# The stretch between attention and the expert tiles in another order

## The reference

```
x = x + layernorm(attention(layernorm(x)))
x = x + layernorm(ffn(layernorm(x)))

# ffn: 7 routed experts of width 512, the best 2 of each token, and one shared
logits = x_flat @ router_w.T
top_vals, top_idx = top_k(logits, 2);  top_w = softmax(top_vals)
mixed = sum over the 2 of top_w * swiglu_expert(x_flat)
mixed = mixed + swiglu_shared(x_flat)
```

## Time and profile before

| | us |
|---|---|
| median of 3 runs | 486.38 |
| lowest and highest run | 486.29, 487.9 |
| the profiled execution | 487.31 |
| its span, first to last instruction | 485.5 |

### The profile page before, as it was taken

The page is one execution under the profiler, slowest core; times in us unless marked ns, Lnnn a source line. Parts: engine busy times, 40 slices in busy tenths (PEclk is TensorE's granted clock), DMA queues, the critical chain, the costliest instruction groups (busy, mean ns, idle before and its releaser), DMA issues. The chain is left out here.

```text
span 485.5 us, 10662 instructions
## 1 busy us (share of the span) xinstructions
PE 416.2 (86%) x3980; PEld 255.0 (53%) x3980; DVE 325.7 (67%) x823; ACT 244.5 (50%) x416; POOL 133.8 (28%) x220
## 2 busy tenths in 40 slices
PE   1869899999999999999989878897999999999500
PEld 0533433435243433435244364655699999999500
DVE  5899978797988888797963936499433333333277
ACT  1531167776777677686776707653233233233240
POOL 8200000100111110100110013334667766763332
PEclk9985589999999999999998959999999999999955
DMA  7554750303021020000000017100577687877152
GB/s 218 198 180 142 244 160 20 90 2 88 3 63 28 11 81 2 2 2 4 1 3 3 0 53 208 44 2 0 169 216 248 209 253 247 238 221 239 43 161 86
DMA packets 46694, 50.77 MB, mean 105 GB/s; under 512 B 5363, under 2 KB 34420, under 8 KB 46644
## 3 DMA queue, kind: packets, MB, share of 16 engines
q1 hardware_dynamic: 43632, 44.77, 30.1%
q0 software_dynamic: 2432, 4.99, 3.6%
q10 hardware_dynamic: 580, 0.33, 0.3%
HBM read 36.90 MB, written 12.98 MB: 103 GB/s over the span
## 5 line engine op out<-in xcount | busy, mean ns | idle before, releaser
L640 ACT ACTIVATE probs<-banks 128x1024 f32<-128x1024 f32 (+1 forms) x192 | 145.3, 810 | 59.1 <-PE banks L495 48.0
L786 DVE TENSOR_REDUCE mx_part<-banks 128x1 f32<-128x512 f32 (+2 forms) x224 | 130.2, 646 | 15.9 <-PE banks L476 7.5
L470 PE MATMUL banks<-k_st,q_st 64*128 64x512 bf16 (+3 forms) x384 | 115.7, 354 | 8.0 <-DVE parts L754 4.2
L488 PE MATMUL banks<-q_st,k_st 64*128 64x512 bf16 (+3 forms) x384 | 97.5, 333 | 6.2 <-ACT probs L640 5.9
L507 PE MATMUL banks<-probs,v_pad 128*32 128x512 f32 (+3 forms) x768 | 83.3, 506 | 0.0
L1525 DVE TENSOR_TENSOR hidden<-banks,gate 128x512 f32<-128x512 f32 x38 | 26.3, 692 | 66.2 <-PE banks L1192 66.2
L488 PEld LDWEIGHTS banks<-q_st,k_st 64*128 64x128 bf16 x384 | 31.1, 95 | 60.9 <-ACT probs L640 49.0
L786 DVE TENSOR_REDUCE mx<-banks 128x1 f32<-128x512 f32 (+3 forms) x96 | 51.9, 596 | 16.5 <-PE banks L476 15.2
L470 PEld LDWEIGHTS banks<-k_st,q_st 64*128 64x128 bf16 x384 | 34.4, 95 | 36.3 <-DVE mx_part L786 27.7
L474 PE MATMUL banks<-mask_qk,ident_half 64*128 64x128 bf16 x256 | 52.6, 231 | 0.0
L493 PE MATMUL banks<-mask_kq,ident_half 64*128 64x128 bf16 x256 | 49.3, 221 | 0.0
(11 more groups left out here) (199 smaller groups left out, 572.2 us busy)
## 6 DMA issues: line engine op xcount, KB each, us to landing
w_g<-in_w_gate SPq DMA_DIRECT2D x38, 256.0 KB
w_u<-in_w_up SPq DMA_DIRECT2D x38, 256.0 KB
q_st<-q_rows SPq DMA_DIRECT2D x32, 128.0 KB, 2.9
k_st<-k_rows SPq DMA_DIRECT2D x32, 128.0 KB, 2.9
w_d<-in_w_down SPq DMA_DIRECT2D x8, 256.0 KB, 5.1
back<-results SPq DMA_DIRECT2D x8, 256.0 KB, 4.7
q_rows<-parts SPq DMA_DIRECT2D x4, 384.0 KB, 3.0
k_rows<-parts SPq DMA_DIRECT2D x4, 384.0 KB, 3.5
```

Source lines behind the costliest of these rows:

```text
L470: last = nc.tensor.matmul(dst[:, at:at + width], q_st[r][rows, c, p, (i % CH) * P:(i % CH + 1) * P], k_st[r][rows, kc, p, 0:width], start= ...
L488: last = nc.tensor.matmul(dst[a][:, 0:width], k_st[r][rows, j // CH, p, (j % CH) * P:(j % CH + 1) * P], q_st[r][rows, c, p, first:BANK], s ...
L640: nc.scalar.activation(probs[unit % PROBS][:, 2 * p:2 * p + 2, first:BANK], slot_pair[k % 2].rearrange("p (a t) -> p a t", a=2)[:, :, 0:BA ...
L786: nc.vector.tensor_reduce(dst, taken[:, :, 0:width], AX.X, ALU.max, negate=True).then_inc(max_taken, 1)
```

## The change

- **End of the first block.** The turns and the routing of batch 0 go to the second block (`first_turn_tokens`, `first_route`, their copies and the logits are gone from the first). VectorE inverts the last group's first sums ahead of the second norm and the last ones right behind x2. NEWTON is 3 instead of 4. ScalarE ends its queue with one more square root of a column nobody reads.
- **Second block.** TensorE turns and routes chunks 0 and 1 behind the projection of batch 1 and ahead of any shared unit; ScalarE copies them. Batch 0's logits have a bank of their own. VectorE takes the statistics of batch 1's projection half by half, and the choice is a function of the batch, `choose(b)`, run for 0 and then 1. The shared units stand elsewhere: three of chunk 0 ahead of chunk 2's and 3's turns, the down projection of each chunk later, three of chunk 2 behind the table. ScalarE has one more unread square root ahead of the second root.
- **Last chunk.** `shared_up(3)`, `shared_take(3)`, `shared_last` and `shared_down(3)` stand behind the tiles; ScalarE copies the result between its scaling of chunk 2 and chunk 3, and GpSimd's adds wait for it. `turn(0)` now stands in front of `shared_down(2)`.

```diff
 RSQRT_BITS = float(0x5F3759DF)
-NEWTON = 4
+NEWTON = 3
 E, HID = 7, 512
...
-            def first_turn_tokens():
-                for q in range(2):
-                    pe.wait_ge(x2_ready, q + 1)
-                    for j in range(CH):
-                        last = nc.tensor.transpose(first_x2_bank[q][:, j * P:(j + 1) * P],
-                                                   x2[:, q * CH + j, :], ident[:, :])
-                    last.then_inc(x2_transposed, 1)
-
-            def first_route():
-                pe.wait_ge(x2_t_ready, 2)
-                for t in range(KT):
-                    last = nc.tensor.matmul(first_lg_bank[:, t * 8:t * 8 + E], x2_t[:, t, :], router_sb[:, :],
-                                            start=True, stop=True)
-                last.then_inc(first_logits_done, 1)
-
             pe.wait_ge(parts_ready, 8)
...
             turn_outputs(GROUPS - 1, 1)
-            first_turn_tokens()
-            first_route()
...
             take_outputs(GROUPS - 1, 1)
+            nc.scalar.activation(std[:, KT:KT + 1], ident[:, 0:1], ACT.Sqrt)
...
                                     ).then_inc(vector_steps, step.one())
+            invert_sums(GROUPS - 1, 0)
             dve.wait_ge(vector_steps, step.now())
...
                     last.then_inc(x2_ready, 1)
-            for q in range(2):
-                dve.wait_ge(x2_transposed, q + 1)
-                nc.vector.tensor_copy(x2_t[:, q * CH:(q + 1) * CH, :].rearrange("p t c -> p (t c)"),
-                                      first_x2_bank[q]).then_inc(x2_t_ready, 1)
-            dve.wait_ge(first_logits_done, 1)
-            nc.vector.tensor_copy(logits[:, 0:KT, 0:E],
-                                  first_lg_bank[:, 0:KT * 8].rearrange("p (t e) -> p t e", e=8)[:, :, 0:E]
-                                  ).then_inc(vector_steps, step.one())
-            invert_sums(GROUPS - 1, 0)
             invert_sums(GROUPS - 1, 1)
...
-            lg_bank, t_out = t_bank[:, 0:cut], t_bank[:, 2 * P:2 * P + 3 * TILES]
+            lg_bank, t_out = [d_bank[:, 0:cut], t_bank[:, 0:cut]], t_bank[:, 2 * P:2 * P + 3 * TILES]
             total_bank = t_bank[:, cut:cut + E * NT]
...
                         pool.wait_ge(weighted, n + 1)
+                        pool.wait_ge(s_down_taken, q + 1)
                         nc.gpsimd.tensor_tensor(mixed[:, part, :], mixed[:, part, :], back[i][:, part, :],
...
                     pe.wait_ge(x2_ready, q + 1)
+                    if q >= 2:
+                        pe.wait_ge(x2_t_ready, q - 1)
                     for j in range(CH):
...
                     for t in range(q * CH, (q + 1) * CH):
-                        last = nc.tensor.matmul(lg_bank[:, t * 8:t * 8 + E], x2_t[:, t, :], router_sb[:, :],
+                        last = nc.tensor.matmul(lg_bank[q // QC][:, t * 8:t * 8 + E], x2_t[:, t, :], router_sb[:, :],
                                                 start=True, stop=True)
...
+                turn_tokens(0)
+                turn_tokens(1)
+                route(0)
+                route(1)
                 pe.wait_ge(shared_loaded, 16 * 3)
                 pe.wait_ge(proj_ready, 2)
-                shared_up(0, range(HT))
-                shared_up(1, [0])
-                shared_down(0)
-                shared_up(1, [1])
+                shared_up(0, [0, 1, 2])
                 turn_tokens(2)
...
                 route(3)
-                shared_up(1, [2, 3])
-                shared_up(2, [0])
-
-                pe.wait_ge(picked_ready, 1)
+                shared_up(0, [3])
+                shared_up(1, [0])
+
+                pe.wait_ge(picked_ready, B)
                 pe.wait_ge(route_consts, 8)
...
                 nc.tensor.matmul(total_bank, ones_b[:, :], flat, start=True, stop=True).then_inc(counted, 1)
-                shared_down(1)
-                shared_up(2, [1, 2, 3])
-                shared_up(3, [0])
-                shared_down(2)
+                shared_down(0)
+                shared_up(1, [1, 2, 3])
+                shared_up(2, [0])
                 for k in range(2 * NT):
+                    if k == NT:
+                        shared_down(1)
                     if k % NT == 0:
...
                 last.then_inc(table_done, 1)
-                shared_up(3, [1, 2, 3])
+                shared_up(2, [1, 2, 3])
...
                 turn(0)
-                shared_down(CHUNKS - 1)
+                shared_down(CHUNKS - 2)
                 turn(1)
...
                 up(0)
-                pe.wait_ge(s_down_taken, CHUNKS)
+                pe.wait_ge(s_down_taken, CHUNKS - 1)
                 for k, e in enumerate(digits(pe)):
...
                     project(k, e)
+
+                shared_up(CHUNKS - 1, range(HT))
+                pe.wait_ge(result_ready, TILES)
+                shared_down(CHUNKS - 1)
...
-                shared_take(0, [0])
+                copy_tokens(0)
+                copy_tokens(1)
                 standard_deviations(0, KT, KT)
-                shared_take(0, [1, 2, 3])
+                shared_take(0, [0, 1])
+                nc.scalar.activation(root_table[:, :], ident[:, 0:1], ACT.Sqrt)
                 standard_deviations(1, KT, KT)
+                copy_tokens(2)
+                copy_tokens(3)
+                shared_take(0, [2, 3])
                 shared_take(1, [0])
                 shared_result(0)
-                shared_take(1, [1])
-                copy_tokens(2)
-                copy_tokens(3)
-                shared_take(1, [2, 3])
+                shared_take(1, [1, 2, 3])
+                act.wait_ge(gap_ready, B)
+                nc.scalar.activation(gap_exp[:, :], gap[:, :], ACT.Exp).then_inc(gap_exp_ready, 1)
                 shared_take(2, [0])
                 shared_result(1)
-                act.wait_ge(gap_ready, 1)
-                nc.scalar.activation(gap_exp[:, :], gap[:, :], ACT.Exp).then_inc(gap_exp_ready, 1)
                 shared_take(2, [1, 2, 3])
-                shared_take(3, [0])
-                shared_result(2)
-                shared_take(3, [1, 2, 3])
...
                         gate_rows(k + 1)
+                shared_take(CHUNKS - 1, range(HT))
                 act.wait_ge(weight_ready, 1)
...
                 for q in range(QC, CHUNKS):
+                    if q == CHUNKS - 1:
+                        shared_result(q)
                     act.wait_ge(returned[q], 32)
...
-                def layer_norm(src, at, count, var_sem, std_sem, n):
+                def layer_norm(src, at, count, var_sem, std_sem, n, halves=None):
...
                     for t in range(at, at + count):
+                        if halves is not None and (t - at) % CH == 0:
+                            dve.wait_ge(halves, (t - at) // CH + 1)
                         nc.vector.bn_stats(stats[:, t, :], src(t)).then_inc(steps, step.one())
...
-                dve.wait_ge(proj_ready, 2)
-                layer_norm(lambda t: proj[:, t - KT, :], KT, KT, post_var_ready, post_std_ready, 1)
+                layer_norm(lambda t: proj[:, t - KT, :], KT, KT, post_var_ready, post_std_ready, 1, proj_ready)
                 for t in range(KT, NT):
...
                         last.then_inc(x2_ready, 1)
-                dve.wait_ge(logits_done, QC)
-                nc.vector.tensor_copy(logits[:, KT:, 0:E],
-                                      lg_bank.rearrange("p (t e) -> p t e", e=8)[:, KT:, 0:E]
-                                      ).then_inc(steps, step.one())
-                done()
-                for t in range(NT):
-                    nc.vector.max(top[:, t, :], logits[:, t, :]).then_inc(steps, step.one())
-                done()
-                nc.vector.tensor_tensor(gap[:, :], top[:, :, 1], top[:, :, 0], ALU.subtract
-                                        ).then_inc(gap_ready, 1)
-                for t in range(NT):
-                    nc.vector.max_index(top_at[:, t, :], top[:, t, :], logits[:, t, :]
-                                        ).then_inc(steps, step.one())
-                done()
-                nc.vector.tensor_copy(top_at_f[:, :, :], top_at[:, :, 0:2]).then_inc(steps, step.one())
-                done()
-                dve.wait_ge(route_consts, 8)
-                for i in range(2):
-                    nc.vector.tensor_tensor(
-                        pick[i][:, :, :], iota[:, 0:E].unsqueeze(2).broadcast_to([P, E, NT]),
-                        top_at_f[:, :, i].unsqueeze(1).broadcast_to([P, E, NT]), ALU.is_equal
-                    ).then_inc(steps, step.one())
-                done()
-                nc.vector.tensor_tensor(picked[:, :, :], pick[0][:, :, :], pick[1][:, :, :], ALU.add
-                                        ).then_inc(picked_ready, 1)
+
+                def choose(b):
+
+                    part = slice(b * KT, (b + 1) * KT)
+                    dve.wait_ge(logits_done, (b + 1) * QC)
+                    nc.vector.tensor_copy(logits[:, part, 0:E],
```

(33 more changed lines are left out.)

5 lines of the change are left out of this document (2 added, 3 removed).

## The result

| | before | after |
|---|---|---|
| median of 7 runs each, us | 486.38 | 481.67 |
| lowest and highest run, us | 486.01, 766.23 (the next highest is 487.9) | 480.81, 484.33 |
| profiled execution, us | 487.31 | 481.67 |
| its span, us | 485.5 | 479.9 |

The ratio after to before is 0.9912, with a 95% interval of 0.9892 to 0.9932: some 4.3 us faster, where 9 were forecast. The seven runs after fall into two groups, 480.81 to 481.67 at a mean granted clock of 0.934 and 483.72 to 484.33 at 0.925 to 0.927; the profile is of the first group, so what sets the second apart is not shown.

What follows compares the result with a forecast made beforehand. Bound: an unbroken chain of waits through the second block, then TensorE's tiles and the results' way home. Front -7.2, up to first tile -2.2, tail +0.3 give -9.1: 487.31 to 478.2, median 477.4; range 473.3 to 481.3.

Steps and rivals of the forecast that it cites:

- The front: End of the first block: the second block's begin (B) was to come 7.2 us earlier, at 280.9.
- x2 at B+16.8: Second block: the second batch's x2 complete 16.8 us behind the block's begin, against 20.15 before.
- The hole's clock: Third down projection: after 5 us idle, TensorE runs 22 of 32 matmuls at half speed, 6.0 us in all.
- rival 4: ScalarE's table switches cost more than their row, 1.28 again each: +1.7, 479.1 us; chance 0.02.
- 5: Tile stage: the fallen clock doesn't come back, making the kernel slower, 504 us if half the stage is affected; chance 0.03.
- from gather to the turn that needs it 2.78: Ahead of the first tile: the first turn follows the first gather by 2.78 us, as before, at 53.5 behind the block's begin.
- the rank matmul starts at B+24.8, 1.0 late: Second block: shared pairs at half clock make the rank matmul 1.0 us late behind picked, bounds 0 and 2.
- 2.2 + 1.0: Between picked and table: GpSimd's products stall VectorE's one-hots by 2.2 us in the first half, 1.0 in the second.
- The table's half: Behind the hot matrices: half of the table's 1.66 us is left, putting the table at 43.1 behind the block's begin.
- +0.3 forecast: Tail: half of the last chunk's 0.6 us ScalarE copy comes through, 0.3 us longer, bounds 0 and 1.8.
- 0.9 of slack: Second root table on ScalarE: ready at 13.25 us behind the block's begin, needed by 14.15.
- Rival 2: Only the front's gain stays: stalls of 5 instead of 3.2, ScalarE late by 1; 479.6 to 481 us; chance 0.18.

Runs made afterwards that it cites:

- newton4: The changed kernel with four Newton steps again in the first block's root instead of three; one profile, 483.43 us.
- weights_later: The changed kernel with SyncE starting the first experts' weight transfers only after the first gather has landed; median 482.14, ratio 0.9908 to the kernel before.
- gathers_ahead: The changed kernel with GpSimd issuing the first two gathers ahead of its last three shared products; median 479.07, ratio 0.9846 to the kernel before.
- rank_first: The changed kernel with the rank and total matmuls ahead of chunk 1's first shared unit; median 482.32, ratio 0.9892 to the kernel before.
- no_products: The changed kernel without GpSimd's four products of chunk 1, ScalarE's copy standing in; median 480.1, ratio 0.9845 to the kernel before.
- turn_behind: The changed kernel with the third down projection ahead of the first turn instead of behind it; median 478.48, ratio 0.9816 to the kernel before.
- fill_hole: The changed kernel with eight unread 128x512 matmuls in TensorE's hole ahead of the first turn; median 482.2, ratio 0.9904 to the kernel before.
- moves_and_units: The changed kernel with earlier gathers and rank matmuls, one unit before the second root table, last chunk's units 0 and 1 before the first turn; 474.89, ratio 0.9766.
- units_in_hole: The changed kernel with the last chunk's gate and up matmuls, silus and VectorE products ahead of the first turn; median 482.42, ratio 0.9925.

## Why the prediction was wrong

**Right.** The front: 7.2 forecast; from the last turn to B it was 10.24 and is 2.88, 7.36 less. x2 at B+16.8: B+16.19. Picked 7.0 behind it: 7.04. From the table's matmuls to the last product 7.1: 7.18 (the chain, 324.58 to 331.76). The hole's clock: 22 of 32 matmuls at half speed forecast, 18 measured, 5.55 for 6.0. GpSimd's product as the last thing ahead of the gather, as said. No table switch cost more than its row: the root table's own root stands at 292.80, 1.30 behind its load at 291.50, so rival 4 didn't come about; nor did 5, since the tiles took 106.58. The saving of two Newton rounds is 1.20 (newton4).

**Luck.** B came another 1.19 earlier by the attention's own time, which no step of the prediction is about. Without it the profile would have missed by more.

**Wrong, by size.** The forecast had the first tile at B+59.9 and it is at B+63.38. In the timeline of before the first weight transfer comes behind the gather of 342.27:

```profile
343.95 0.38 SPq L1004 DMA_DIRECT2D w_g<-in_w_gate  x1
```

1. The step "from gather to the turn that needs it 2.78": 5.22, +2.44. I took the price from a gather that stood 1.68 ahead of the first weight transfer, and never asked what moving it behind GpSimd's products would put in front of it. SyncE's queue hangs on `words` alone, and its first issue is now 2.48 ahead of the gather. weights_later shows the cause (2.81 with the transfers held back), gathers_ahead too (2.84 with the gather first). This is the largest term.
2. The step "the rank matmul starts at B+24.8, 1.0 late": 2.07 late, +1.07. The pairs ahead of it ran at 1.91 and 1.71 for two matmuls (the chain above), as the clock fell later than I had it and came back only in 303:304, 9 behind TensorE's first turn of 294.77 instead of the 4.9 that I had counted from there. It is just past the bound of 2 that I had named. rank_first removes it, and shows that only 0.6 of it is to be had.
3. "2.2 + 1.0" for VectorE's stalls: the stretch from the rank matmul to the hot matrices took 18.55 for 17.4, +1.15. The first half of the hot matrices cost 0.7 more than charged, the slots 0.55, for which no stall was charged beyond what 5.95 held; no_products puts the whole price of the products at 4.9.
4. The table's half 1.18 for 0.9, +0.28. Against these stand x2, the issue behind the product and the down projection, 0.6, 0.3 and 0.6 better than forecast. With 0.1 for picked and the last product, 2.44 + 1.07 + 1.15 + 0.28 + 0.1 - 1.5 = +3.5.

**Wrong, in the tail.** +0.3 forecast, +1.47 measured. Some 0.4 is ScalarE's copy. The other 1.0 is the landing of the results' loads: ScalarE could begin 12.01 behind E for 10.97 before, and 11.1 to 12.4 over all the profiles. Their cause stays open: leaving out the last chunk gave 10.74 in the single profile taken, but the profiles with it differ among themselves by more than the 1.0.

**Missed altogether.** "0.9 of slack" at the second root table was 0.1 even at full clock: the new root ended at B+13.45, 0.2 later than forecast, and var_eps 0.6 earlier than the B+14.15 that I had allowed. And the forecast never counted the first pairs at half clock. When they run at half the load is 2.05 late and x2 with it, +1.8 to +2.4. Five of the profiles show it (turn_behind, no_products, weights_later, fill_hole, rank_first); after's own doesn't, so it is no part of the +3.5.

Rival 2 (stalls of 5, ScalarE late by 1) named two of these mechanisms and gave 479.6 to 481; the measured median, 481.67, is above that and 0.4 above the range. It lacked the gather.

## What to carry to other kernels

A transfer's price belongs to its place in the order of all queues: when a gather moves behind something, look for what another queue issues in the meantime. Slack that rests on TensorE's pace is to be counted at 1.2 GHz too wherever a hole stands ahead of it. Work that has to be done anyway can fill a hole of TensorE: in moves_and_units it kept the clock up and brought the first tile 1.5 forward. That it also pays at the place it left was not seen, as the tail stayed as long (27.07 for 27.00, and 28.17 in units_in_hole).

## What the runs showed of the hardware

- An indirect gather took 5.11 us to land with five weight transfers of 256 KB issued up to 2.5 us ahead of it (after). With SyncE holding them back it landed in 2.71 (weights_later), and the turn stood 2.78 to 2.84 behind the gather wherever it came first (before, gathers_ahead).
- The granted clock fell (0.73 in 335:336) just behind a hole of only 2.07 us, 332.78 to 334.86, in turn_behind. It also fell with TensorE at work: in after in 296:297 (0.92), with PE busy 1.00 in turns and routing matmuls, 2 us behind the end of a hole of 2.20 and 1 us behind a second of 0.37. But it stayed at full over the hole of 2.93 ahead of 318.55 in after. So the length of the hole alone doesn't tell, as far as these rows go.
- after and weights_later are the same up to SyncE's wait for the gather, some 40 us later; the clock was at full in 289:290 in one and at half in the other.
- VectorE's tensor_scalar on 128x608 bf16 took 0.38 alone (no_products) and 1.27 beside a GpSimd product of 128x512 f32 (after); its row_hot of 128x2048 2.28 and 3.35, and the product up to 1.81 instead of 1.27 in after, up to 2.95 in rank_first.
